# Gate and up products of a mixture of experts: three float32r products of split operands, or one float32 product

## The reference, cut to what matters

```
h2 = rmsnorm(hidden, ffn_norm_w)
tok = h2.reshape(T, D)
probs = softmax(tok @ gate_w.T)
topv, topi = top_k(probs, 2)
combine = zeros((T, E)).at[arange(T)[:, None], topi].set(topw)
eg = einsum('td,eid->eti', tok, wg)
eu = einsum('td,eid->eti', tok, wu)
eo = einsum('eti,edi->etd', silu(eg) * eu, wd)
moe_out = einsum('te,etd->td', combine, eo)
```

## Time and profile before

| what | value |
|---|---|
| median of 3 runs | 1172.72 us (1172.37 to 1172.80) |
| the profiled execution's own time | 1174.76 us |
| its span in the trace | 1172.9 us |
| PE busy | 1141.4 us, 97% of the span |
| DVE / ACT / POOL busy | 725.7 / 645.5 / 506.7 us |

### The profile page before, as it was taken

How to read it: one execution, slowest core, us unless ns; L and a number is a source line. 1 busy time by engine, 2 the same in 40 slices (tenths; PEclk the granted TensorE clock), 3 DMA queues, 4 the chain that set the end, 5 groups by cost and what they waited for, 6 DMA issues and landing times.

```text
span 1172.9 us, 22331 instructions
## 1 busy us (share of the span) xinstructions
PE 1141.4 (97%) x7602; PEld 1018.7 (87%) x7637; DVE 725.7 (62%) x1587; ACT 645.5 (55%) x1840; POOL 506.7 (43%) x566
## 2 busy tenths in 40 slices
PE   8999999999999999999999999999999999998995
PEld 7989999999999999998997788888888888877994
DVE  3666554334543454347777877777777787766556
ACT  4545543444444443455565766766766666674552
POOL 4111131113111311311336775675677588674573
PEclk9999999999999999999999999999999999999998
DMA  9200000000000002014002008930000100023747
GB/s 345 77 1 1 19 2 18 1 1 1 1 19 1 1 1 91 1 46 171 19 18 73 1 1 227 293 93 1 10 20 10 48 18 19 20 69 91 205 111 244
DMA packets 47265, 70.07 MB, mean 60 GB/s; under 512 B 4279, under 2 KB 39355, under 8 KB 46171
## 3 DMA queue, kind: packets, MB, share of 16 engines
q1 hardware_dynamic: 43475, 59.69, 16.8%
q0 software_dynamic: 3408, 8.43, 2.0%
q10 hardware_dynamic: 272, 0.52, 0.1%
HBM read 40.24 MB, written 29.30 MB: 59 GB/s over the span
## 4 chain that ended last, share of the span: by engine, by line
PE 89%; DVE 4%; issue 2%; ACT 2%; POOL 2%; DMA 1%; SPq 0%; POOLq 0%; DVEq 0%; ACTq 0%
PE bank L1878 15%; PE bank L1915 11%; PE bank L2068 10%; PE bank L1946 8%; PE bank L2122 7%; PE bank L1888 5%; PE bank L2213 5%; PE bank L1906 5%; PE bank L2148 4%; PE bank L2008 3%; PE bank L2256 3%; PE bank L2283 3%; PE bank L1896 2%; PE bank L2188 2%; PE bank L2178 2%
## 5 line engine op out<-in xcount | busy, mean ns | idle before, releaser
L592 POOL TENSOR_TENSOR p<-p,rinv 128x512 f32<-128x512 f32 x64 | 66.6, 1040 | 403.5 <-DVE rinv L1424 403.5
L946 ACT ACTIVATE p<-bank,nb,rq 128x128 f32<-128x128 f32 x256 | 113.8, 454 | 89.2 <-DVE nb L1647 89.2
L813 ACT ACTIVATE p<-bank,nmax 128x128 f32<-128x128 f32 x256 | 90.5, 366 | 115.6 <-DVE nmax L1412 115.4
L667 POOL TENSOR_TENSOR qr<-qr,rb 128x512 f32<-128x512 f32 x64 | 82.5, 1289 | 72.1 <-DVE rb L1601 70.6
L1420 DVE COPY pt<-bank 128x512 f32<-128x512 f32 x64 | 44.2, 691 | 106.0 <-PE bank L1896 105.4
L1878 PE MATMUL bank<-cur_hi,wqk_hi 128*128 128x512 f32 x256 | 107.8, 421 | 0.6 <-DVE cur_lo L1361 0.6
L1878 PE MATMUL bank<-cur_lo,wqk_hi 128*128 128x512 f32 x256 | 101.1, 395 | 0.0
L1878 PE MATMUL bank<-cur_hi,wqk_lo 128*128 128x512 f32 x256 | 100.9, 394 | 0.0
L822 ACT ACTIVATE o_hi<-bank,bqkv 128x512 fp32r<-128x512 f32 x64 | 44.2, 690 | 95.9 <-PE bank L1906 95.5
L1428 DVE SCALAR_TENSOR_TENSOR o_lo<-bank,bqkv,o_hi 128x512 fp32r<-128x512 f32 x64 | 48.0, 750 | 49.6 <-ACT o_hi L822 49.6
L1915 PE MATMUL bank<-wo_hi,o_hi 128*128 128x256 f32 x256 | 77.7, 303 | 0.3 <-DVE o_lo L1428 0.2
(11 more groups left out here) (274 smaller groups left out, 3652.4 us busy)
## 6 DMA issues: line engine op xcount, KB each, us to landing
token_scratch<-empty SPq DMA_DIRECT2D x1, 17415.0 KB, 64.8
xs<-token_scratch SPq DMA_DIRECT2D x39, 129.0 KB
wqk_raw<-in_wqk SPq DMA_DIRECT2D x8, 512.0 KB, 9.8
gate<-gates_scratch SPq DMA_DIRECT2D x8, 512.0 KB, 3.8
got_t<-expert_scratch SPq DMA_DIRECT2D x16, 256.0 KB, 4.8
w_raw<-in_w SPq DMA_DIRECT2D x2, 1408.0 KB, 6.0
xres<-in_x SPq DMA_DIRECT2D x4, 512.0 KB, 8.9
wv_raw<-in_wv SPq DMA_DIRECT2D x8, 256.0 KB, 10.0
```

The source lines that it names most:

```text
L592: nc.gpsimd.tensor_tensor(p1[:, h % 2], p1[:, h % 2], rinv[:, h % 2].unsqueeze(2).broadcast_to([P, GB, T]), ALU.mult).then_inc(a_pn, 1)
L667: nc.gpsimd.tensor_tensor(qr[:, s.u % 2], qr[:, s.u % 2], rb[:], ALU.add).then_inc(g_qr, 1)
L813: last = nc.scalar.activation(p1[:, h % 2, b], bank[3][:, b * T:(b + 1) * T], ACT.Exp, bias=nmax[:, h % 2, b:b + 1], accum_out=rsum[:, h % ...
L946: last = nc.scalar.activation(p2[:, (s.u - 3) % 2, j], bank[3][:, j * T:(j + 1) * T], ACT.Exp, scale=rq[:, (s.u - 3) % 4, j:j + 1], bias=n ...
```

## The change

The weights `w3` are loaded as they are and stay float32. Nobody splits them: ACT's L995 and L1000, DVE's L1729 and POOL's L709 are gone. ACT's copy of bank 0 (`x_out`) writes float32 `xt`; DVE's `x_lo` is gone. `gate_up` issues two products with plain float32 operands in place of six with float32r operands. The waits of PE on `e_xl` become waits on `e_xh`, ACT's copy; `goals` on DVE now carries the wait on `e_xh`, which `x_lo` had. `gate_up(0)` waits for the two loads of `w3` rather than for their splitting.

```
-        w3_hi = [sb("w3_hi0", [P, E, 2 * I], F32R, at=W), sb("w3_hi1", [P, E, 2 * I], F32R, at=W + 64 * KB)]
-        w3_lo = [sb("w3_lo0", [P, E, 2 * I], F32R, at=W + 11 * KB), sb("w3_lo1", [P, E, 2 * I], F32R, at=early + 4 * KB)]
-        w3_raw = [sb("w3_raw0", [P, E, 2 * I], at=W + 11 * KB), sb("w3_raw1", [P, E, 2 * I], at=early + 4 * KB)]
+        w3 = [sb("w3_0", [P, E, 2 * I], at=W + 11 * KB), sb("w3_1", [P, E, 2 * I], at=early + 4 * KB)]
...
-                if s.g == NG - 1 and W31_STEP <= s.u < W31_STEP + 4:
-
-                    for t in (2 * (s.u - W31_STEP), 2 * (s.u - W31_STEP) + 1):
-                        pool.wait_ge(w_hi4, E + t + 1)
-                        nc.gpsimd.tensor_tensor(w3_lo[1][:, t], w3_raw[1][:, t], w3_hi[1][:, t].bitcast(F32),
-                                                ALU.subtract).then_inc(w_lo4p, 1)
...
-            def x_lo(i):
-
+            def goals(i):
+
+                c = i % NX
                 dve.wait_ge(e_xh, i + 1)
-                if i >= 2:
-                    dve.wait_ge(e_gu, i - 1)
-                nc.vector.tensor_tensor(xt_lo[:, i % 2], bank[0][:, 0:D],
-                                        xt_hi[:, i % 2].bitcast(F32), ALU.subtract).then_inc(e_xl, 1)
...
-                    pe.wait_ge(e_xl, i)
+                    pe.wait_ge(e_xh, i)
...
                 for k in range(KD):
-                    hi, lo = (w[k][:, bass.ds(e, 1), :].rearrange("p a n -> p (a n)") for w in (w3_hi, w3_lo))
-                    for j, (l, r) in enumerate(split_products(xt_hi[:, i % 2, ks[k]], xt_lo[:, i % 2, ks[k]], hi, lo)):
-                        last = pe.matmul(bank[1 + i % 2][:, 0:2 * I], l, r, start=(k == 0 and j == 0),
-                                         stop=(k == KD - 1 and j == 2))
+                    last = pe.matmul(bank[1 + i % 2][:, 0:2 * I], xt[:, i % 2, ks[k]],
+                                     w3[k][:, bass.ds(e, 1), :].rearrange("p a n -> p (a n)"), start=(k == 0), stop=(k == KD - 1))
```

More of the change, by code:

```diff
@@ L239, in program @@
         xs = sb("xs", [P, NX, DW], at=W + 75 * KB)
-        xt_hi = sb("xt_hi", [P, 2, KD * P], F32R, at=place["cur_hi"][0])
-        xt_lo = sb("xt_lo", [P, 2, KD * P], F32R, at=place["cur_hi"][0] + 2 * KB)
+        xt = sb("xt", [P, 2, KD * P], at=place["cur_hi"][0])
         ht = sb("ht", [IC, 2, 2 * P], at=place["cur_lo"][0])
@@ L310, in program @@
             sem(f"g_{x}") for x in ("ka", "rk", "kv", "qr", "rq", "qv", "pn"))
-        w_hi4, w_lo4 = sem("w_hi4"), sem("w_lo4")
-        e_xp, e_xh, e_xl, e_gu, e_sg, e_h, e_hp, e_hh, e_dp, e_o = (
-            sem(f"e_{x}") for x in ("xp", "xh", "xl", "gu", "sg", "h", "hp", "hh", "dp", "o"))
+        e_xp, e_xh, e_gu, e_sg, e_h, e_hp, e_hh, e_dp, e_o = (
+            sem(f"e_{x}") for x in ("xp", "xh", "gu", "sg", "h", "hp", "hh", "dp", "o"))
         t_lg, t_ex, t_v0, t_v, t_cb = (
@@ L317, in program @@
         s_rank, s_v = sem("s_rank"), sem("s_v")
-        w_lo4p, s_goal = sem("w_lo4p"), sem("s_goal")
+        s_goal = sem("s_goal")
         r_in, m_y = sem("r_in"), sem("m_y")
@@ L460, in _ @@
             sp.wait_ge(f_dp, NG * NF)
-            sp.dma_start(w3_raw[0][:], ins["w3"][0]).then_inc(d_w3[0], 16)
+            sp.dma_start(w3[0][:], ins["w3"][0]).then_inc(d_w3[0], 16)
             sp.dma_start(rw[:], ins["rw"]).then_inc(d_router, 16)
@@ L468, in _ @@
             sp.wait_ge(c_lo, KD * 3 * NG)
-            sp.dma_start(w3_raw[1][:], ins["w3"][1]).then_inc(d_w3[1], 16)
+            sp.dma_start(w3[1][:], ins["w3"][1]).then_inc(d_w3[1], 16)
             def load_tile(i):
@@ L991, in step @@
                     split_out(NG - 1)
[L992 to L1000, removed]
                 if s.u == 4 * GB + 2:
@@ L1004, in step, with x_out @@
                     expert(s.u - DRAIN[TILES])
-            def x_hi(i):
+            def x_out(i):
                 act.wait_ge(e_xp, i + 1)
@@ L1010, in x_hi @@
                     act.wait_ge(e_gu, i - 1)
-                nc.scalar.activation(xt_hi[:, i % 2], bank[0][:, 0:D], ACT.Copy).then_inc(e_xh, 1)
+                nc.scalar.activation(xt[:, i % 2], bank[0][:, 0:D], ACT.Copy).then_inc(e_xh, 1)
             def gate_silu(i):
@@ L1045, in expert @@
                 if i < NT:
-                    x_hi(i)
+                    x_out(i)
                 if i == 8 - TILES:
@@ L1724, in step @@
                     list0[s.u - 1]()
[L1725 to L1730, removed]
                 if s.u == 4 * GB + 5:
@@ L1749, in step @@
                         nc.vector.bn_stats(bn[:, b], xres[:, BA + b])
-            def x_lo(i):
-                dve.wait_ge(e_xh, i + 1)
-                if i >= 2:
-                    dve.wait_ge(e_gu, i - 1)
-                nc.vector.tensor_tensor(xt_lo[:, i % 2], bank[0][:, 0:D],
-                                        xt_hi[:, i % 2].bitcast(F32), ALU.subtract).then_inc(e_xl, 1)
             def goals(i):
                 c = i % NX
+                dve.wait_ge(e_xh, i + 1)
                 if i in (0, T1, T2):
@@ L1798, in expert @@
                 if i < NT:
-                    x_lo(i)
                     goals(i)
@@ L2243, in gate_up @@
                 if i == 0:
-                    pe.wait_ge(w_lo4, E)
-                    pe.wait_ge(w_lo4p, E)
+                    pe.wait_ge(d_w3[0], 16)
+                    pe.wait_ge(d_w3[1], 16)
                     pe.wait_ge(g_kt, B)
@@ L2248, in gate_up @@
                     pe.wait_ge(s_v, S_PLACE0[NG - 2] + 1)
-                pe.wait_ge(e_xl, i + 1)
+                pe.wait_ge(e_xh, i + 1)
                 if i >= 2:
```

2 lines of the change are left out of this document (removed).

## The result

| what | before | changed |
|---|---|---|
| median of 9 runs each, same chip | 1173.26 us (1171.57 to 1175.23) | 1177.57 us (1175.36 to 1179.90) |
| ratio changed to before, 95% interval | | 1.0037 (1.0026 to 1.0048) |
| the profiled execution's own time | 1174.76 us | 1178.98 us |

The change makes the kernel slower by 0.37%, some 4.3 us (3.1 to 5.6 us by the interval). The forecast was 1175.2 us. The sign and the side of 0.2% came as forecast as likeliest; the size was larger than the +2.5 us of the sum. In the profiled execution the excess lies in its first 16 us, 1000 us ahead of the changed products.

A forecast was written before the change was run, and what follows sets the result against it. PE, busy 97% of the span, was taken as the bound. Products +8.55, splitting -1.0, standing -2.6 and clock -2.4 us in timed runs gave +2.5 us, 1175.2 us; range 1172.0 to 1179.0.

The forecast's parts named there:

- The products: Gate and up in the expert tiles: two float32 products instead of six, 0.219 us more a tile, 8.55 us for 39.
- The splitting of `w3`: Second attention: without the hi and lo writes, two waits shrink, a gain of 1.0 us.
- the first group: Second attention: without DVE's `w_lo` ahead of `nmax`, PE's 1.42 us wait at the scores ends 0.43 us earlier.
- The drain: End of second attention: `nb` no longer slowed beside POOL's `w_lo`, a gain of 0.6 us, between 0.1 and 0.8.
- a further 0.1 us from the step before: Preceding step of the drain, with POOL's `w_lo` in the same place: 0.1 us beyond the 0.48 us coming back.
- Standing and clock among the first tiles: First expert tiles without DVE's `xt_lo`: 2.6 us less standing, 2.8 us by a held clock (2.4 in timed runs).
- the rows' wait: PE's wait for the normalised rows among the first tiles: 1.4 us of standing in place of 0.8 + 0.9.
- the picks: PE's wait for the router's picks among the first tiles: 0.35 us left of 0.96.
- `h`: Behind routing on DVE, next in line after the second `xt_lo` wait: 0.4 us of standing.
- The rival of the clock: First tiles: the clock falls all the same, so 2.4 us don't come: +4.9 us, 1177.6 us; chance 0.22.
- `xt` wait: PE's two waits for `xt_lo` from 1055 us on, 0.64 and 1.56 us, both forecast to go.

The follow-up runs named there:

- changed_sends_spread: Changed kernel with POOL's eight last-group sends issued two by two in expert(7) to expert(10): 1190.03 us against 1189.38 for the kernel before, ratio 0.9998.
- changed_mended: Changed kernel with those sends two by two and DVE's last tile-list parts behind the normalisation sums: 1188.26 us, 0.9988 of the kernel before.
- changed_again: Changed kernel with no edit, rerun on another chip: 1187.84 us against 1187.89 for the kernel before, ratio 1.0007.

## Why the prediction was right, and where not

**The products: right.** Forecast 0.219 us a tile, 2.49 us from `wd` to `wd`, 0.297 us a record; measured 0.216 us, 2.49 us and 1.19 / 4 = 0.297 us. Two rows of the same type at other widths, 256 and 512 columns, gave the price at 352 within the reading of the trace. That nothing hides it from 1090 us on held too: 70.00 of 70.00 us busy.

**The splitting of `w3`: the two places right, a third one missed, too small a price (1.38 us for 1.0).** At the place forecast the first group gave 0.41 us of the 0.43; DVE, then ACT, then PE came earlier by just that:

```profile
658.27 0.68 DVE L1622 TENSOR_REDUCE nmax<-bank 128x4 f32<-128x512 f32 x1
...
659.06 0.17 DVE L1626 TENSOR_TENSOR nb<-nmax,rq 128x4 f32<-128x4 f32 x1
```

A second wait of that group, at 692 us, was 0.16 us that the forecast didn't have. It hides under the end of PE's own record, so no list of waits has it; it shows only in the distance to the next start, before and then after:

```profile
688.76 0.52 DVE L1729 TENSOR_TENSOR w_lo<-w_raw,w_hi 128x352 fp32r<-128x352 f32 x1
...
691.59 0.60 PE L2188 MATMUL bank<-ident,p 128*128 128x128 f32 x4
692.19 0.38 PE L2210 MATMUL bank<-mask,ident_b 128*128 128x512 bf16 x1
```

```profile
693.70 0.60 PE L2153 MATMUL bank<-ident,p 128*128 128x128 f32 x4
694.14 0.38 PE L2175 MATMUL bank<-mask,ident_b 128*128 128x512 bf16 x1
```

The scores come 0.60 us behind the turnings before and 0.44 us after.

The drain gave 0.81 us for 0.6, at the upper bound of 0.8. The larger part is as forecast: `nb` takes 0.16 us where it took 0.65, and PE's wait went from 0.90 to 0.42 us.

```profile
1046.00 0.16 DVE L1626 TENSOR_TENSOR nb<-nmax,rq 128x4 f32<-128x4 f32 x1
...
1048.43 0.83 PE L2178 MATMUL bank<-k_t,q_t 128*128 128x128 f32 x6 [0.42 <-ACT p L934]
```

The other 0.32 us is PE's wait in the step before, which went altogether. The failed term is "a further 0.1 us from the step before". I had sized it by what `nb` loses there to POOL (0.28 us, now 0.16: 0.12 us). The other 0.2 us is that DVE comes to `nmax` of that step earlier, at 1039.16 us before and 1040.90 after, which is 1.74 us later where PE is 1.95 us later. One step earlier still `nb` took 0.76 us beside POOL's `w_lo` and takes 0.16 after; that this is what brings DVE forward is likely and not tested. For the long `nb` the traces bear out the reason: it took 0.65 us beside POOL's `w_lo` and ended at 1045.03 us, 0.03 us behind the first of POOL's two operations (0.95 us from 1044.05 on), and with `w_lo` gone it takes 0.16 us.

**Standing and clock among the first tiles: right.** From the drain to `wd` of tile 6 the changed kernel gained 3.33 us with nine longer tiles in it: 3.33 + 9 x 0.219 = 5.3 us, against 2.6 + 2.8 = 5.4. Step by step: the rows' wait is 1.3 us (in a trace's counting; forecast 1.4 with the 0.16 us that a record runs on), the picks 0.2 (0.35 with them), `h` 0.06 (some 0.25 with them, by the starts) instead of 0.4. No `xt` wait is left. `h` starts at 1082.06 us and PE turns it at 1082.44:

```profile
1082.06 0.33 DVE L1738 TENSOR_TENSOR h<-sg,bank 128x176 f32<-128x176 f32 x1
...
1082.44 0.42 PE L2231 MATMUL bank<-ident,h 128*88 128x128 f32 x2
```

**The rival of the clock fell.** It let the clock fall behind the rows' wait. The wait is there and turnings stand behind it, and the clock is at 1.00 from 1057 to 1160 us:

```profile
1069.75 1.06 PE L1803 MATMUL bank<-ident,rows 128*128 128x128 f32 x8 [1.28 <-DVE rows L1077]
```

```profile
1066.00:1072.00 6.00, 4.72 (x26) 3.29 (x25) 3.41 (x11) 2.51 (x7) 3.85 (x6) 1.00 0.30 89
```

That is 1.28 us idle, then eight turnings up to 1070.8 us, and the clock held. The start of the kernel before has turnings alone as well, behind 1.66 us without work: 28 of them, 0.21 us apart up to 4.9 us and 0.11 us apart from then on, with a granted clock of 1.00 in both stretches. What halved the distance isn't shown. The time near that rival's 1177.6 us comes from elsewhere, so whoever had only the time would have taken the rival for right.

**What the forecast lacked: the start.** 2.5 us of the profiled difference, more than half, lie in the first 15 us. The sum had no term for that since the code there isn't changed, and the range took it in only by its other terms. Is it the change, or luck? Among the traces of the changed kernel and its variants the long `xn` shows in three of seven (3.40 to 3.48 us: this one, `changed_sends_spread`, `changed_mended`), in those of before and its variants in none of seven. It isn't POOL's start alone: in `changed_again` POOL starts at 8.71 us and `xn` keeps its 1.38 us. One with the collision, from `changed_mended`, and one without, from `changed_again`:

```profile
7.68 3.48 DVE L1060 TENSOR_SCALAR xn<-xres,mv,rstd 128x256 f32<-128x256 f32 x4 [1.44 <-POOL rstd L546]
...
8.67 2.34 POOL L555 TENSOR_TENSOR wqk_lo<-wqk_raw,wqk_hi 128x1024 fp32r<-128x1024 f32 x1 [1.03 <-ACT wqk_hi L775]
```

```profile
7.64 1.38 DVE L1060 TENSOR_SCALAR xn<-xres,mv,rstd 128x256 f32<-128x256 f32 x4 [1.44 <-POOL rstd L546]
...
8.71 2.53 POOL L555 TENSOR_TENSOR wqk_lo<-wqk_raw,wqk_hi 128x1024 fp32r<-128x1024 f32 x1 [1.11 <-ACT wqk_hi L775]
```

With 0.04 us between them, it looks like a race of the last `xn` with POOL, and all fourteen traces fit: from the start of the first `xn` to that of `wqk_lo` are 0.86, 0.95 and 0.99 us in the three with the long `xn`, and 1.03 to 1.70 us in the eleven others. The price shows as well. The first scores of the second attention start at 643.4 to 644.0 us in the three; in the others they start at 640.3 to 640.9 us, or at 641.3 to 641.6 us where the clock fell at 9 us. The nine times of the changed kernel on the first chip lie in two heaps with one between: four from 1175.36 to 1176.09 us with a mean clock of 0.995 or 0.996, at the forecast's 1175.2, one at 1177.57 and four from 1178.98 to 1179.90 with 0.992 or 0.993. The profiled one, with the collision, is in the upper heap. The six profiled executions of the changed kernel and its variants on the other chips fit that too: the two with the collision are in the upper half of their own kernel's times, the four without in the lower half. So it is plausible that the upper heap has the collision and the lower doesn't; it isn't shown, as only one of the nine has a trace here. Whether the change makes the collision likelier (three of seven against none of seven is too little to tell) stays open. If it doesn't, the change is worth about +2 to +2.6 us on this chip (+1.9 us by the traces, and 1175.85, the middle of the lower heap, less 1173.26).

**On the other chips** the forecast would have been too high: +0.8 and +0.2 us. Its premise, that only DVE's work makes PE stand among the first tiles, doesn't hold where ACT stops.

## What to carry to other kernels

Price a product by the pitch of rows with the same type at neighbouring widths: here that held to a hundredth of a us (0.2966 us a record forecast, 0.297 measured). The waits around it need "what is late next" one by one, in every step of a chain and not only where the longest wait stands. Edits that shorten work ahead of the same wait need not add: measured alone, `xt_lo` was worth 4.9 us, and together with longer products 2.1. After a run, go through the difference from the start with the same instruction in both traces: more than half of this one lay in code that nobody had touched, and the total alone would have confirmed the wrong rival.

## What the runs showed of the hardware

- A DVE `tensor_scalar` with one SBUF input, writing float32, was held up until a POOL `tensor_tensor` was over: 3.44 instead of 1.38 us for four of them, ending 0.15 us behind POOL's instruction. In fourteen traces it was held in the three where POOL started 0.86 to 0.99 us behind the first of the four, and not in the eleven where it started 1.03 to 1.70 us behind. In the changed kernel's trace it cost 1.7 us at once and, as an estimate from the 2.5 us that stayed, some 0.8 more by a clock that was at 0.50 for 3.4 us.
- ACT stopped by itself for some 12 us in all among the first expert tiles in the twelve traces from the other chips, and not in the two from the first. PE then stood about 2 and, for the most part, 4 to 5 us, and behind the second stop the clock was at 0.50 for 3.4 to 13.7 us. The DMA share was no higher there than on the first chip (0.36 and 0.40 against 0.30 to 0.77), and neither the sends nor the products moved it. Its cause isn't settled.
- The length of a wait alone didn't say whether the granted clock would fall. A wait of 1.28 us followed by eight turnings of 128x128 left it at 1.00, and waits of 2.79 and 4.68 us went with 0.50. But behind waits of about 2 us that end at 1061 to 1065 us it fell in six traces and held in six, and behind the wait for `xn` at 9 us it fell in three traces with waits of 0.45 to 0.63 us and held in eight with 0.20 to 0.86.
- Turnings with nothing else on PE came 0.21 us apart up to 4.9 us and 0.11 us apart from then on, 28 of them at the start of the kernel before, at a granted clock of 1.00 throughout.
